# Two-layer graph network and mixture of experts: the router one tile slot earlier, two tiles picked at once and loaded three slots ahead, rows normalised in place, and another order of the lead groups

## The chip, the cores and the metric

One core of a Trainium2 chip. The metric is the device time of one launch in microseconds; the median of three runs stands for the kernel.

## The reference, cut to what matters

`x` has 10000 rows (nodes, later tokens) of 512 numbers. Two relational graph layers come first, then a mixture of experts on the normalised result.

```python
h   = relu(rgcn_gate_layer(layernorm(x), ...))        # x @ root + bias + sum over 5000 edges
x   = x + rgcn_gate_layer(h, ...)                      # second layer
t   = layernorm(x)
shared = sum over 2 experts of gelu(t @ sw1.T + sb1) @ sw2.T + sb2
probs  = softmax(t @ gate_w.T + gate_b)                # 8 routed experts
top_v, top_i = top_k(probs, 2)                         # the two best, with their shares
routed = sum over those two of top_v * (gelu(t @ rw1.T + rb1) @ rw2.T + rb2)
x   = x + shared + routed
```

## The kernel before, in words

**Stages.** The two graph layers take the first 931 us of the span: node tiles of 128 rows through `root`, 42 edge tiles through the relation weights, results added to `y1` and `z` in DRAM. The last 11 node tiles of layer 2 ("late2", loop over `late2_steps`) are multiplied after the edges. Then comes the mixture of experts, and that is where the change lies.

**Groups.** Tokens go through the router in 20 groups `q` of 512 (4 tiles of 128 rows in a partition). `load_group` (SP's queue) loads `x` into `zr`, `add_z` (POOL's queue, an accumulating DMA) adds `z`; `q_stats` (DVE) takes mean and variance; `group_rstd` (POOL) the factors; `q_norm` (ACT) writes the normalised rows to `stage`; `q_transpose` (PE) with `q_full` (ACT) turns them; `logits` and `logits_by_token` (PE), with `q_logits` (ACT) between them, give 8 logits for each token; `route_a`, an exponential in `q_exp` (ACT) and `route_b` (DVE) give the two best shares; `sort_kinds` (DVE) says which of 6 kinds (pairs of expert halves) a token is of; `count_ranks` (PE) counts ranks; `positions` (DVE) gives each token its row in the DRAM table `sorted_rows`, and `sort_rows` (POOL, 4 indirect DMAs) writes the rows there.

**Slots.** The experts work on 45 tiles of 256 sorted rows, one in each slot `i`. `pick_tile` (DVE) picks the kind with most rows; `load_tile` (SP) waits for the pick and for the sorting of all groups that it may read, and loads `xt[i % 4]`. A slot has `turn_tile` (transposes of the tile, PE; `f_hi`/`f_lo` split them on ACT and DVE), `up_routed` (26 matmuls), `up_shared` (12), the Gelu on ACT, `weigh` on DVE, `turn_hidden` (4 transposes), `down_first` (8), `down_routed` (12), `f_out` on DVE and `store_tile` (POOL, 2 indirect DMAs to `out`). PE's order in a slot is up_routed, up_shared, turn_tile of the next tile, [logits, counts, two q_transposes], turn_hidden, down_first, the third part of turn_tile, [two q_transposes, logits_by_token], down_routed.

**What sets the order.** Each engine runs its own list in program order; semaphores tie them. Groups 0 to 4 (lead groups) are routed before slot 0, partly between late2 steps. Groups 5 to 19 share the slots: every second slot turns, ranks and sorts one, so two slots and one group make a pair. `group_at(i, offset)` gives the group whose turn a step is in slot `i`; the last group is ranked in slot 31, and slots 32 to 44 have no group. The picks for slots `i + 2` and `i + 3` are made in the odd slot `i` that ranks a group, and `load_tile` is called two slots ahead:

```python
for i in range(NF):
    if exists(i + 2):
        load_tile(i + 2)
```

In the late2 steps DVE makes the router's small tables (`router_tiles`, which waits until the last edge rows are scattered) in step 2 and takes group statistics in steps 3, 5 and 8.

Of the kernel before, what the change touches and what calls it, by code (L numbers as in the profile page):

```python
# [63 lines left out]
def gnn_moe_kernel(nc, x, src, dst, etype, basis, att, gate_w, root, bias,  # L64
# [60 lines left out]
    with ctx:  # L125
# [63 lines left out]
        gbias = sb("gbias", [P, NE])  # L189
# [6 lines left out]
        kinds = sb("kinds", [P, 5, NKIND])  # L196
        rank_base = sb("rank_base", [P, QT, NKIND])
        lim_base = sb("lim_base", [P, NKIND])
        limt_base = sb("limt_base", [P, NKIND])
# [59 lines left out]
        zr, z1 = place("zr", [P, 2, QT, H], at=q1)  # L259
# [4 lines left out]
        seen = sb("seen", [P, 2, NKIND], BF16)  # L264
        is_kind = sb("is_kind", [P, 3 + QT, NKIND], BF16)
        pos = sb("pos", [P, 3, QT], I32)
        lim = sb("lim", [P, 2, NKIND])
        limt = sb("limt", [P, 2, NKIND])
        pick = sb("pick", [P, NF, 5])
# [3 lines left out]
        pick_one = sb("pick_one", [P, NKIND])  # L273
        pick_all = sb("pick_all", [P, 5, NKIND])
# [3 lines left out]
        stage, g1 = place("stage", [P, 3, QT, XW], at=xe_at)  # L278
# [19 lines left out]
        lgs = sb("lgs", [P, QT, NE])  # L298
# [4 lines left out]
        lg = sb("lg", [P, QT, NE])  # L303
        lg2 = sb("lg2", [P, QT, NE])
        mx = sb("mx", [P, QT])
        ex = sb("ex", [P, QT, NE])
        sm = sb("sm", [P, QT])
        rc = sb("rc", [P, QT])
        pr = sb("pr", [P, QT, NE])
        mx8 = sb("mx8", [P, QT, 8])  # L310
        topv = sb("topv", [P, QT, 8])
        rest = sb("rest", [P, QT, NE])
        cw = sb("cw", [P, QT, NE])
        cwh = sb("cwh", [P, QT, NE], F32R)
        qvar = sb("qvar", [P, 2, QT])
        held = sb("held", [P, QT, 4])
        has = sb("has", [P, QT, 4])
        half = sb("half", [P, QT, 2])
        newly = sb("newly", [P, NKIND])
# [83 lines left out]
        s_zin = [sem(f"x_loaded{i}") for i in range(2)]  # L403
        s_zadd = [sem(f"z_added{i}") for i in range(2)]
# [15 lines left out]
        s_sorted = [sem(f"rows_sorted{i}") for i in range(3)]  # L420
# [138 lines left out]

        LATE2_GROUP = NC * P // (QT * P)  # L560
# [26 lines left out]
        def turned_in_slot(i):  # L587
            return group_at(i, 9)

        def routed_in_slot(i):  # L590
            q = (i + 8) // 2
            return q if i % 2 == 0 and LEAD_GROUPS - 1 <= q < NQ else None

        def ranked_in_slot(i):
            q = (i + 7) // 2
            return q if i % 2 == 1 and LEAD_GROUPS - 1 <= q < NQ else None

        def picked_in_slot(i):

            q = ranked_in_slot(i)  # L600
            if q is not None:
                return [t for t in (i + 2, i + 3) if t < NF]
            return [i + 3] if i >= 2 * NQ - 8 and i + 3 < NF else []

        TURNS = [("a", 0), ("b", 0), ("x", 0)]
        for slot in range(NF):
            q = turned_in_slot(slot)
            TURNS += [("a", slot + 1), ("b", slot + 1)] if slot + 1 < NF else []
            TURNS += [(0, q), (1, q)] if q is not None else []
            TURNS += [("g", slot)]  # L610
            TURNS += [("x", slot + 1)] if slot + 1 < NF else []
            TURNS += [(2, q), (3, q)] if q is not None else []
# [8 lines left out]
        def wait_turn_bank(eng, part, n):  # L621
# [5 lines left out]
            if place_ < 3:  # L627
                eng.wait_ge(s_lo, 2 * (NT + ET))
                return
# [23 lines left out]
        def _(sp):  # L653
# [113 lines left out]
            def load_moe_small():  # L767
                sp.dma_start(gw[:], moe_gate_wT.rearrange("(k p) e -> p k e", p=P)).then_inc(s_sm2, 16)
                sp.dma_start(gbias[:], moe_gate_b.rearrange("(a e) -> a e", a=1).to_broadcast([P, NE])).then_inc(s_sm2, 16)
# [47 lines left out]
            def load_group(q):  # L817
                wait(sp, s_qn, QT * (q - 1))
                sp.dma_start(zr[:, q % 2, 0:tiles_of(q), :], q_rows(x, q)).then_inc(s_zin[q % 2], 16)

            def load_tile(i):
                q = group_of_pick(i)
                sp.wait_ge(s_pick, i + 1)
                for k in range(3):
                    wait(sp, s_sorted[k], 16 * sum(tiles_of(n) for n in range(k, q + 1, 3)))
# [9 lines left out]
            load_group(0)  # L835
            load_up_experts()
            load_group(1)
            for g in range(NG - 1, NG + 1):
                sp.wait_ge(s_tp, Step(SE, Pos(2 * (g - 4) + 1)).T.k + 1)
                load_pair(SE, Pos(g))  # L840
            for q in range(2, 6):
                load_group(q)
# [3 lines left out]
            load_tile(1)  # L846
            for i in range(NF):
                if exists(i + 2):
                    load_tile(i + 2)
                q = group_at(i, 14)  # L850
                if q is not None and q > 6:
                    load_group(q)
# [5 lines left out]
        def _(pool):  # L858
# [20 lines left out]
            pool.wait_ge(s_pool, 10)  # L879
# [13 lines left out]
            pool.wait_ge(s_pool, 15)  # L893
# [7 lines left out]
            pool.wait_ge(s_pool, 19)  # L901
            pool.sem_inc(s_const, 1)

            def kind_tables():
# [6 lines left out]
                iota(rank_base[:], [[0, QT], [KIND, NKIND]], HEAD + FW)  # L911
                iota(lim_base[:], [[KIND, NKIND]], HEAD)
                iota(limt_base[:], [[1, NKIND]], 0)
# [3 lines left out]
                iota(again_row[:], [[1, QLAST]], 0, QLAST)  # L917
                for k, (a, b, slot) in enumerate(KINDS):
                    for row, value in ((1, slot), (2, a + 1), (3, b + 1)):
                        pool.memset(kinds[:, row, k:k + 1], float(value)).then_inc(s_pool, 1)  # L920
                pool.wait_ge(s_pool, 19 + 26)
                pool.tensor_scalar(limt_base[:], limt_base[:], 0.125, None, ALU.mult).then_inc(s_pool, 1)
                same_rows = QT * P * (NQ - 1) - (N - QLAST * P)
                pool.tensor_scalar(valid[:], again_row[:], float(same_rows), None, ALU.is_ge).then_inc(s_pool, 1)
                pool.wait_ge(s_pool, 19 + 28)
                pool.tensor_tensor(limt_base[:], limt_base[:], lim_base[:], ALU.add).then_inc(s_pool, 1)
                pool.wait_ge(s_pool, 19 + 29)
# [141 lines left out]
            def group_extras(q):  # L1069
                s, n = q % 2, tiles_of(q)  # L1070
                high, low = (stage[:, q % 3, 0:n, SHARES + 3 * NR2 - 2 + k] for k in range(2))
                mean = qmv[:, s, 0:n, 0]
                if q < 3:
                    pool.wait_ge(s_qs, 1)
                else:
                    pool.wait_ge(s_sorted[q % 3], 16 * QT * (q // 3))
                pool.tensor_tensor(stage[:, q % 3, 0:n, STD], qvar[:, s, 0:n], qrstd[:, s, 0:n], ALU.mult).then_inc(s_qx, 1)
# [4 lines left out]
            def add_z(q):  # L1082
                if q == LATE2_GROUP:
                    late2_added(pool)
                pool.wait_ge(s_zin[q % 2], 16 * (q // 2 + 1))
                pool.dma_start(zr[:, q % 2, 0:tiles_of(q), :], q_rows(z, q),
                               accum_op=ALU.add).then_inc(s_zadd[q % 2], 16)

            def sort_rows(q):
                s, n = q % 2, tiles_of(q)  # L1090
                pool.wait_ge(s_qpos, q + 1)
                tokens = stage[:, q % 3, 0:n, TOKEN]
# [6 lines left out]
                for j in range(n):  # L1099
                    pool.indirect_dma_start(out=sorted_rows, in_=stage[:, q % 3, j, :], in_offset=None,  # L1100
                                            out_offset=bass.IndirectOffsetOnAxis(ap=pos[:, q % 3, j:j + 1], axis=0))\
                        .then_inc(s_sorted[q % 3], 16)
# [21 lines left out]
            add_z(0)  # L1124
            add_z(1)
            add_late2(LATE2_PAIRS[0])
            group_rstd(0)
            group_extras(0)
            add_late2(LATE2_PAIRS[1])
            group_rstd(1)  # L1130
            group_extras(1)
            add_z(2)
            add_late2(LATE2_PAIRS[2])
            add_late2(LATE2_PAIRS[3])
            add_z(3)
            group_rstd(2)
            add_late2(LATE2_PAIRS[4])
            sort_rows(0)
# [1132 lines left out]
```

## Time and profile before

| | us |
|---|---|
| median of 3 runs (lowest, highest) | 1766.83 (1765.28, 1771.9) |
| the profiled execution | 1758.73 |
| its span | 1757.0 |
| PE busy in the span | 1523.2 (87%) |
| DVE, ACT, POOL busy | 963.2, 711.8, 655.9 |

The profile is of one execution. The span runs from the first to the last instruction; 1.7 us of the execution lie around it. Slots are told apart by the Gelu of line 1355, one in each slot.

### The profile page before, as it was taken

The numbers are of one execution on the slowest core, as the hardware profiler recorded it, in microseconds if no ns is written. First come the engines' busy times: TensorE is split into PE (matmuls) and PEld (weight loads), VectorE is DVE, ScalarE is ACT, GpSimd is POOL, SyncE is SP. The second block draws the span as 40 slices with busy tenths as digits, with TensorE's granted clock in tenths as the row PEclk, the third lists the DMA queues.
The fourth block names the chain that finished last, engine by engine and source line by source line (L and its number), as shares of the span: only waits on it lengthen the run. The fifth ranks groups of instructions, "written<-read, shape, count | busy, mean of one in ns | idle before, by whom it ended". The sixth has DMA issues, their size and how long they took to land. (4 is left out here: it accounts for less than half of the span.)

```text
span 1757.0 us, 27836 instructions
## 1 busy us (share of the span) xinstructions
PE 1523.2 (87%) x8640; PEld 1216.1 (69%) x8640; DVE 963.2 (55%) x2837; ACT 711.8 (41%) x1232; POOL 655.9 (37%) x988
## 2 busy tenths in 40 slices
PE   7999999889979999999996736788788778878997
PEld 5777667777856777788875525676676667767886
DVE  5555777767523333466643565566465556645553
ACT  3334345556511112256652433454354345432331
POOL 3752142567530000026653344344334434432222
PEclk9999999999999999999998868999899999999999
DMA  9999997977689999967768855555545545432220
GB/s 245 272 282 306 281 308 231 292 133 121 95 200 288 280 278 278 300 187 124 136 105 185 204 162 163 162 159 155 181 132 173 175 148 156 132 103 98 100 75 17
DMA packets 115238, 325.96 MB, mean 186 GB/s; under 512 B 17244, under 2 KB 17770, under 8 KB 109859
## 3 DMA queue, kind: packets, MB, share of 16 engines
q1 hardware_dynamic: 77202, 211.19, 40.5%
q0 software_dynamic: 37904, 113.12, 28.0%
q8 instruction: 70, 1.15, 0.3%
q14 instruction: 62, 0.50, 0.1%
HBM read 205.63 MB, written 121.74 MB: 186 GB/s over the span
## 5 line engine op out<-in xcount | busy, mean ns | idle before, releaser
L1192 ACT ACTIVATE th<-bank 128x512 fp32r<-128x512 f32 x158 | 94.1, 596 | 284.8 <-PE bank L1467 284.6
L1120 POOL DMA_INDIRECT out<-xt,out_row x90 | 91.9, 1021 | 187.9 <-DVE xt L2169 169.6
L1812 DVE SCALAR_TENSOR_TENSOR tl<-bank,th 128x512 fp32r<-128x512 f32 x79 | 54.5, 690 | 190.9 <-ACT th L1192 190.8
L1447 PE MATMUL bank<-root2h,th 128*128 128x512 f32 x316 | 134.5, 425 | 18.3 <-DVE tl L1812 15.6
L984 POOL DMA_INDIRECT gx<-y,dst_slot x42 | 45.4, 1082 | 266.5 <-ACT xn_e L1212 242.6
L1447 PE MATMUL bank<-root1h,th 128*128 128x512 f32 x316 | 133.2, 422 | 7.2 <-DVE yout L1841 4.5
L1447 PE MATMUL bank<-root2l,th 128*128 128x512 f32 x316 | 127.2, 402 | 0.0
L1447 PE MATMUL bank<-root1l,th 128*128 128x512 f32 x316 | 126.5, 400 | 0.0
L1447 PE MATMUL bank<-root2h,tl 128*128 128x512 f32 x316 | 126.2, 400 | 0.0
L1447 PE MATMUL bank<-root1h,tl 128*128 128x512 f32 x316 | 125.6, 397 | 0.0
L1614 PE MATMUL bank<-ident,xt 128*128 128x128 f32 x360 | 57.7, 313 | 77.1 <-DMA xt<-sorted_rows 77.1
L1841 DVE TENSOR_TENSOR yout<-bank,bias_b 128x512 f32<-128x512 f32 x152 | 103.7, 682 | 26.2 <-DMA y<-yout 10.3
L1815 DVE TENSOR_TENSOR tl<-bank,th 128x512 fp32r<-128x512 f32 x79 | 54.4, 689 | 93.6 <-ACT th L1192 93.0
L1614 PEld LDWEIGHTS bank<-ident,xt 128*128 128x128 f32 x360 | 47.6, 161 | 80.6 <-DMA xt<-sorted_rows 80.6
L1447 PE MATMUL bank<-w1qh,tth 128*128 x360 | 101.6, 282 | 1.0 <-DVE ttl L2149 1.0
L1447 PE MATMUL bank<-w1ql,tth 128*128 x360 | 101.9, 283 | 0.0
L1447 PE MATMUL bank<-w1qh,ttl 128*128 x360 | 101.9, 283 | 0.0
L1480 PE MATMUL bank<-same,eh 128*128 128x256 f32 x336 | 84.3, 288 | 16.9 <-issue 9.2
L2149 DVE TENSOR_TENSOR ttl<-bank,tth 128x512 fp32r<-128x512 f32 x90 | 59.1, 685 | 72.3 <-ACT tth L1344 71.5
L999 POOL DMA_INDIRECT z<-msg,scat_slot x42 | 70.5, 1678 | 64.1 <-issue 64.1
L1100 POOL DMA_INDIRECT sorted_rows<-stage,pos x79 | 81.0, 1025 | 27.4 <-issue 14.2
L1355 ACT ACTIVATE gelr<-bank 128x512 f32<-128x512 f32 x45 | 26.9, 598 | 157.3 <-PE bank L1633 157.2
(292 smaller groups left out, 4490.3 us busy)
## 6 DMA issues: line engine op xcount, KB each, us to landing
basis_t<-in_gnn_basis SPq DMA_DIRECT2D x64, 896.0 KB
xt<-sorted_rows SPq DMA_DIRECT2D x45, 560.0 KB, 4.0
xin<-in_x SPq DMA_DIRECT2D x39, 512.0 KB, 8.7
xin<-y SPq DMA_DIRECT2D x39, 512.0 KB, 8.1
zr<-in_x SPq DMA_DIRECT2D x19, 1024.0 KB, 5.2
zr<-z POOLq DMA_DIRECT2D x19, 1024.0 KB, 8.1
y<-yout SPq DMA_DIRECT2D x37, 512.0 KB, 8.9
z<-yout SPq DMA_DIRECT2D x34, 512.0 KB, 7.7
```

What stands on the lines that cost most here:

```text
L984: pool.indirect_dma_start(out=gx[:, e % 6, :], out_offset=None, in_=x if pr.phase == SB else y1, in_offset=bass.IndirectOffsetOnAxis(ap=ds ...
L999: pool.indirect_dma_start(out=y1 if pr.phase == SB else z, out_offset=bass.IndirectOffsetOnAxis(ap=scat_slot[:, t:t + 1], axis=0), in_=msg ...
L1100: pool.indirect_dma_start(out=sorted_rows, in_=stage[:, q % 3, j, :], in_offset=None, out_offset=bass.IndirectOffsetOnAxis(ap=pos[:, q % 3 ...
L1120: pool.indirect_dma_start(out=out, in_=xt[i % 4][:, j, 0:H], in_offset=None, out_offset=bass.IndirectOffsetOnAxis(ap=out_row[:, i % 4, j:j ...
L1192: act.activation(th_a[:, s, :], tpb[s][:], f).then_inc(s_hi, 1)
L1447: ins = pe.matmul(out_ap, a(k), b(k), start=first, stop=last)
L1480: pe.matmul(o, eh[:, j, k * P:(k + 1) * P], m, start=j == 0, stop=False)
L1614: ins = pe.transpose(b[:, k * FW + j * P:k * FW + (j + 1) * P], t[:, j, (first + k) * P:(first + k + 1) * P], ident[:])
L1812: ins = dve.scalar_tensor_tensor(out=tl_a[:, s, :], in0=tpb[s][:], scalar=0.0, in1=th_a[:, s, :].bitcast(F32), op0=ALU.max, op1=ALU.subtract)
L1815: ins = dve.tensor_tensor(tl_a[:, s, :], tpb[s][:], th_a[:, s, :].bitcast(F32), ALU.subtract)
L1841: dve.tensor_tensor(target, out_bank(st)[:], bias_b[st.layer][:], ALU.add).then_inc(s_y, 1)
L2149: dve.tensor_tensor(to[0], turn_bank(part, i)[:], to[1].bitcast(F32), ALU.subtract).then_inc(s_flo, 1)
```

## The change: what it does

- `ranked_in_slot` gives a group to the even slot `(i + 8) // 2` instead of the following odd one; `routed_in_slot` moves to the odd slot before it, `turned_in_slot`, statistics, loads and adds move one slot earlier relative to the group. The two picks of a group are for slots `i + 3` and `i + 4`, and `load_tile` is called three slots ahead.
- `zr` goes. `x` and `z` are loaded and added straight into four `stage` buffers of 560 numbers a row, the statistics are taken there, and `q_norm` works in place. `load_group` waits for the sorting of the group four before.
- The router bias is added in `q_logits`; the top two are taken from the logits and the exponential is taken of both the logits and the logits without the top two; the tensor `seen` of counts goes, running limits are kept in `lim` by DVE. `route_a` has one more step (max and match), `route_b` and `sort_kinds` have fewer.
- PE's order in a slot becomes up_routed, count_ranks, two q_transposes, logits, up_shared, turn_hidden, turn_tile of the next tile, logits_by_token, down_first, two q_transposes, down_routed 0, third part of turn_tile, the register loads of the next pick, down_routed 1. In ACT's list `q_full` 0 and 1 and `q_logits` stand behind the first Gelu, `routed_hi` ahead of `f_hi`. In DVE's `positions` stands behind `weigh`, `routed_lo` ahead of `f_lo`, `route_a`, picks, `route_b` and `sort_kinds` at the end.
- Lead groups: all four loads and adds go ahead of late2's adds; `router_tiles` is in late2 step 5, statistics in steps 6 and 8 (and the others behind the last), group 0 is turned ahead of step 9; groups 1 to 3 follow step 10, with `positions(q - 1)` behind `route_a(q)`; group 4 is turned and routed ahead of slot 0 and ranked in it.

```diff
         def turned_in_slot(i):
-            return group_at(i, 9)
+            return group_at(i, 10)
 
         def routed_in_slot(i):
-            q = (i + 8) // 2
-            return q if i % 2 == 0 and LEAD_GROUPS - 1 <= q < NQ else None
+            return group_at(i, 9)
 
         def ranked_in_slot(i):
-            q = (i + 7) // 2
-            return q if i % 2 == 1 and LEAD_GROUPS - 1 <= q < NQ else None
+            q = (i + 8) // 2
+            return q if i % 2 == 0 and q < NQ else None
...
-                return [t for t in (i + 2, i + 3) if t < NF]
-            return [i + 3] if i >= 2 * NQ - 8 and i + 3 < NF else []
+                return [t for t in (i + 3, i + 4) if t < NF]
+            return [i + 4] if i > 2 * NQ - 10 and i + 4 < NF else []
...
             def load_group(q):
-                wait(sp, s_qn, QT * (q - 1))
-                sp.dma_start(zr[:, q % 2, 0:tiles_of(q), :], q_rows(x, q)).then_inc(s_zin[q % 2], 16)
+                wait(sp, s_sorted[q % 4], 16 * QT * (q // 4))
+                sp.dma_start(stage[q % 4][:, 0:tiles_of(q), 0:H], q_rows(x, q)).then_inc(s_zin[q % 4], 16)
...
-                if exists(i + 2):
-                    load_tile(i + 2)
+                if exists(i + 3):
+                    load_tile(i + 3)
...
             def q_norm(q):
                 s = q % 2
                 act.wait_ge(s_qst, q + 1)
-                wait(act, s_sorted[q % 3], 16 * QT * (q // 3))
-                wait(act, s_qtp, KC * (q - 1))
...
-                    act.activation(stage[:, q % 3, j, 0:H], zr[:, q % 2, j, :], ACT.Identity, bias=qnmr[:, s, j:j + 1],
+                    act.activation(rows, rows, ACT.Identity, bias=qnmr[:, s, j:j + 1],
...
                 ins.then_inc(s_upr, 1)
-                up_shared(i)
-                if exists(i + 1):
-                    turn_tile(i + 1, "a")
-                    turn_tile(i + 1, "b")
-                if q_route is not None:
-                    logits(q_route)
                 if q_rank is not None:
                     count_ranks(q_rank)
                 if q_turn is not None:
                     q_transpose(q_turn, 0)
                     q_transpose(q_turn, 1)
+                if q_route is not None:
+                    logits(q_route)
+                up_shared(i)
                 turn_hidden(i)
-                chunks = [pe.value_load(pick_int[0:1, i, c:c + 1], min_val=1, max_val=FC - 1) for c in (2, 3)]
+                if exists(i + 1):
+                    turn_tile(i + 1, "a")
+                    turn_tile(i + 1, "b")
+                if q_route is not None:
+                    logits_by_token(q_route)
                 for j in range(2):
                     down_first(i, j)
-                if exists(i + 1):
-                    turn_tile(i + 1, "x")
                 if q_turn is not None:
                     q_transpose(q_turn, 2)
                     q_transpose(q_turn, 3)
-                if q_route is not None:
-                    logits_by_token(q_route)
-                for j in range(2):
-                    down_routed(i, j, chunks)
+                down_routed(i, 0, chunks)
+                if exists(i + 1):
+                    turn_tile(i + 1, "x")
+                    chosen = picked(i + 1)
+                down_routed(i, 1, chunks)
...
-                if e == 2:
+                if e == 5:
                     router_tiles()
-                if e in (3, 5, 8):
-                    q_stats({3: 0, 5: 1, 8: 2}[e], range(QT))
...
+                if e == 6:
+                    q_stats(0, range(QT))
+                if e == 8:
+                    q_stats(1, range(QT))
...
                 for t in picked_in_slot(i):
                     pick_tile(t)
...
                 if q_route is not None:
-                    route_a(q_route)
                     route_b(q_route)
+                    sort_kinds(q_route)
```

## Rows read from the trace of the kernel before

**Rows 1.** The page: span, and PE's busy tenths in 40 slices of 43.9 us.

```profile
span 1757.0 us, 27836 instructions
...
PE   7999999889979999999996736788788778878997
```

**Rows 2.** Busy time of each engine by stretch, granted clock, DMA share, GB/s.

```profile
955.00:1010.00 55.00, 37.76 (x173) 27.97 (x173) 28.46 (x87) 21.15 (x35) 18.25 (x31) 0.79 0.87 202
1010.00:1053.00 43.00, 15.73 (x96) 10.13 (x94) 28.58 (x145) 15.23 (x28) 18.18 (x30) 0.64 0.61 166
...
1105.00:1605.00 500.00, 407.96 (x2643) 341.14 (x2641) 288.60 (x1158) 223.39 (x381) 200.66 (x363) 0.94 0.49 149
1300.30:1333.60 33.30, 27.30 (x178) 22.70 (x178) 19.48 (x79) 15.36 (x26) 14.01 (x25) 0.95 0.54 165
...
1650.00:1694.50 44.50, 43.84 (x291) 39.39 (x291) 22.82 (x64) 13.33 (x28) 11.90 (x25) 1.00 0.26 86
```

**Rows 3.** The Gelu of line 1355, slots 0 to 10 and 32 to 44.

```profile
L1355 ACT ACTIVATE gelr<-bank x11: 597/598/598, 1068.5 to 1230.8; 128x512 f32<-128x512 f32 x11
...
L1355 ACT ACTIVATE gelr<-bank x13: 598/598/598, 1601.2 to 1739.0; 128x512 f32<-128x512 f32 x13
```

**Rows 4.** Waits from 1105 to 1605 us: total, times, longest.

```profile
PEld bank L1614 <- DMA xt<-sorted_rows: 61.6, 14, 5.6
```

**Rows 5.** DMA issues of the same stretch: count, KB, median us to landing.

```profile
xt<-sorted_rows SPq DMA_DIRECT2D x28, 560.0 KB, 4.4
...
zr<-z POOLq DMA_DIRECT2D x11, 1024.0 KB, 8.1
...
sorted_rows<-stage,pos POOLq DMA_INDIRECT x59, 4.2
```

**Rows 6.** PE in one pair of slots: start, us, what, idle before.

```profile
1304.43 1.22 PE L1614 MATMUL bank<-ident,xt 128*128 128x128 f32 x8 [4.13 <-DMA xt<-sorted_rows]
1305.58 1.93 PE L1581 MATMUL bank<-tfull,gwp 128*32 128x512 f32 x8
```

**Rows 7.** ACT in the same pair.

```profile
1311.16 1.28 ACT L1338 ACT_TABLE_LOAD   x1
...
1313.03 2.94 ACT L1319 ACTIVATE stage<-zr,qnmr,qrstd 128x512 f32<-128x512 f32 x4 [0.34 <-POOL qnmr L1067]
```

**Rows 8.** DVE in the same pair.

```profile
1311.20 0.29 DVE L2056 TENSOR_REDUCE lgs<-bank 128x32 f32<-128x128 f32 x1 [0.27 <-PE bank L1588]
...
1317.97 0.17 DVE L2109 TENSOR_TENSOR seen<-seen,newly 128x6 bf16<-128x6 bf16 x1
1319.36 0.76 DVE L2155 TENSOR_TENSOR gelr<-gelr,xt 128x256 f32<-128x256 f32 x2 [1.22 <-issue]
```

**Rows 9.** PE in a slot without a group.

```profile
1657.95 0.28 PE L1447 MATMUL bank<-w1qh,tth 128*128 x1
...
1661.06 0.28 PE L1447 MATMUL bank<-tth,w1sh 128*128 128x256 f32 x1
...
1662.51 1.03 PE L1614 MATMUL bank<-ident,xt 128*128 128x128 f32 x8
1663.38 0.60 PE L1646 MATMUL bank<-ident,gelr 128*128 128x128 f32 x4
1664.12 0.50 PE L1655 MATMUL bank<-b2r,cwt 128*128 128x512 f32 x1
...
1666.22 0.48 PE L1447 MATMUL bank<-w2h,grh 128*128 x1
```

**Rows 10.** DVE in such a slot: its first operation.

```profile
1662.02 0.76 DVE L2155 TENSOR_TENSOR gelr<-gelr,xt 128x256 f32<-128x256 f32 x2 [3.12 <-ACT gelr L1355]
```

**Rows 11.** PE from late2 to slot 0: first instruction after three long idle times.

```profile
955.51 0.80 PE L1447 MATMUL bank<-root2h,th 128*128 128x512 f32 x1 [10.54 <-DVE tl L1812]
...
1045.59 1.12 PE L1588 MATMUL bank<-ident,lgt 128*128 128x128 f32 x4 [10.91 <-ACT lgt L1333]
...
1069.90 1.97 PE L1614 MATMUL bank<-ident,xt 128*128 128x128 f32 x8 [11.56 <-DMA xt<-sorted_rows]
```

More of the change, by code:

```diff
@@ L823, in load_tile @@
                 sp.wait_ge(s_pick, i + 1)
-                for k in range(3):
-                    wait(sp, s_sorted[k], 16 * sum(tiles_of(n) for n in range(k, q + 1, 3)))
+                for k in range(4):
+                    wait(sp, s_sorted[k], 16 * sum(tiles_of(n) for n in range(k, q + 1, 4)))
                 if i < 4:
@@ L1332, in q_logits @@
                 wait(act, s_lgx, q)
[L1333 removed]
+                act.activation(lgt[:, 0:n], bank[7][:, 0:n], ACT.Identity, bias=gbias[:, 0:1]).then_inc(s_lgt, 1)
             def q_exp(q):
@@ L1409, in _ @@
             f_shares(0)
+            for k in range(KC):
+                q_full(4, k)
+            q_logits(4)
+            q_exp(4)
             q_norm(5)
@@ L2101, in sort_kinds @@
[L2101 to L2104 removed]
+                left = held[:, 0:n, 0:2].rearrange("p j (a b) -> p j a b", b=1).to_broadcast([P, n, 2, 2])
@@ L2180, in _ @@
                     expert_lo(FC + e - 2)
-                if e == 2:
+                if e == 5:
                     router_tiles()
-                if e in (3, 5, 8):
-                    q_stats({3: 0, 5: 1, 8: 2}[e], range(QT))
-                if e == 7:
-                    route_a(0)
-                    route_b(0)
-                    sort_kinds(0)
-                if e == 9:
-                    positions(0)
-            for q in range(1, 4):
-                route_a(q)
-                if q < 3:
-                    q_stats(q + 2, range(QT))
-                route_b(q)
-                sort_kinds(q)
-                if q < 3:
-                    positions(q)
-                if q == 2:
-                    pick_tile(0)
-                    bias_rows()
-            for part in ("a", "b"):
-                f_lo(0, part)
+                if e == 6:
+                    q_stats(0, range(QT))
+                if e == 8:
+                    q_stats(1, range(QT))
+            q_stats(2, range(QT))
+            route_a(0)
+            route_b(0)
+            sort_kinds(0)
+            q_stats(3, range(QT))
+            route_a(1)
+            positions(0)
+            route_b(1)
+            sort_kinds(1)
+            route_a(2)
+            positions(1)
+            route_b(2)
+            sort_kinds(2)
+            route_a(3)
+            positions(2)
+            pick_tile(0)
+            route_b(3)
+            sort_kinds(3)
+            bias_rows()
             positions(3)
@@ L2206, in _ @@
             pick_tile(2)
+            q_stats(4, range(QT))
+            for part in ("a", "b"):
+                f_lo(0, part)
+            route_a(4)
             q_stats(5, range(QT))
+            route_b(4)
+            sort_kinds(4)
             for i in range(NF):
-                q_route, q_rank, q_first, q_more = routed_in_slot(i), ranked_in_slot(i), group_at(i, 11), group_at(i, 10)
+                q_route, q_rank, q_first, q_more = routed_in_slot(i), ranked_in_slot(i), group_at(i, 12), group_at(i, 11)
                 if i:
@@ L2212, in _ @@
                         f_out(i - 1, j)
-                if q_rank is not None and q_rank > 3:
-                    sort_kinds(q_rank)
                 if q_more is not None and q_more > 5:
-                    q_stats(q_more, range(1, 3))
+                    q_stats(q_more, range(2, QT))
                 chunks = [dve.value_load(pick_int[0:1, i, c:c + 1], min_val=1, max_val=FC - 1) for c in (2, 3)]
@@ L2219, in _ @@
                     weigh(i, c, chunks[c])
+                if q_rank is not None:
+                    positions(q_rank)
                 shared_lo(i)
+                routed_lo(i)
                 if exists(i + 1):
@@ L2223, in _ @@
                     f_lo(i + 1, "b")
-                routed_lo(i)
-                if q_rank is not None:
-                    positions(q_rank)
+                if q_route is not None:
+                    route_a(q_route)
                 for t in picked_in_slot(i):
```

402 lines of the change are left out of this document (187 added, 215 removed).

## The prediction

> **What bounds the kernel now.** I read the page first: PE is busy 87% of the span, but its row of tenths is at 9 in most slices of the graph layers, falls to 6, 7, 3 in the three slices from about 922 us and stays at 7 or 8 for the next thirteen, then 9 again [rows 1]. So two stretches have slack, and the change touches only these. The table by stretch gives their size: from 1105 to 1605 us PE is busy 408.0 of 500 us at a granted clock of 0.94, DVE 58%, ACT 45%, POOL 40%; from 1650 us, in slots without a group, PE is busy 43.84 of 44.5 us at clock 1.00 [rows 2]. Nothing is saturated in the first and PE is in the second: the first is a latency loop. The Gelu of line 1355 marks the slots: slot 0 at 1068.5, slot 32 at 1601.2, slot 44 at 1739.0 us [rows 3]. So 32 slots took 532.7 us, 33.3 a pair of slots with a group; the last 12 took 137.8.
>
> Which wait ends last? PE's weight loads waited 61.6 us for `xt<-sorted_rows` in 14 pairs, up to 5.6 us each [rows 4]; in the pair I follow the wait was 4.13 us, and the transposes and logits behind it ran slow (8 transposes 1.22, logits 1.93 us; 8 transposes at full clock take 1.03) [rows 6, 9]. The tile is late for a reason seen in the code: `positions` of the odd slot, 4 sort DMAs of about 1.3 us issue each, 4.2 us until the last lands, then 4.4 us for the tile [rows 5], and PE wants the tile in the next slot.
>
> **The pair after the change.** PE's own work first. In a slot without a group [rows 9]: up_routed 1657.95 to 1661.06, 3.11; up_shared 1.45; 8 transposes and turn_hidden 1.61; down_first with the third part 2.10, so about 0.235 a matmul and 2.82 for the 12 of down_routed; sum 11.1 us. A group adds 16 transposes (8 in 0.87), 1.75; logits, half of the slow 1.93, 0.97; 4 transposes 0.44; counts about 0.15 by my estimate (bounds 0 and 0.5): 3.3. Pair: 2 x 11.1 + 3.3 = 25.5 us. Cross-check: the pair before was 27.30 busy [rows 2], and the two slow pieces above hold 1.3 of it, so 26.0. I take 25.5.
>
> Does the tile come in time? From the start `U` of the work behind up_routed in the even slot: `positions` ends near U + 4.5; POOL first stores the tile before (2.6), computes rows (1.2) and issues an add (1.0), then sorts (tokens 0.7, 4 x 1.3), last issue near U + 10.5, landed U + 14.7; SP's registers 1.0; tile landed near U + 20. PE turns tile `i + 3` in slot `i + 2`, near U + 29.5. Nine us to spare, so the 61.6 us go, and with them the slow pieces. The ring through the group's own loads is as safe: `load_group` now waits for the sorting of the group four before, then load (about 5), add 8.1 [rows 5], statistics and turn, some 25 us of DMA and queue for a distance of eight slots, 105 us. Writing rows of 2048 bytes at a pitch of 2240 in place of 8192 bytes in a run costs the loads something that no row shows; bounds 0 and 4 us each (double the 4.4 us of a tile, which is in runs of 4480), hidden by the same 7 to 9 us.
>
> What is late next? The exponential. In the odd slot PE turns the tile's third part only behind half of down_routed. From there to the next turn_hidden ACT has: share copy 0.4, table load 1.28, exp 0.23, q_norm 2.94, table load 1.28, Gelu 0.60 [rows 3, 7], then DVE's weigh 0.76 [rows 8], with 0.3 of handovers 7.8 us. PE has down_routed 1 1.41, up_routed 3.11, counts 0.15, two q_transposes 0.87, up_shared 1.45 = 7.0. Stall 0.8 us. DVE's way round is near the same: from route_a to the end of the kinds 1311.20 to 1318.14 = 6.9 us, less f_out's 1.4 and a wait of 0.5, 5.0 of work [rows 8]; about 2.1 of it (route_b, sort_kinds) follows the exp, then f_out 1.4, register loads 1.22, weigh 0.76, with copy, load, exp and handover 2.0 ahead: 7.4. The kinds are ready 4.2 us after the third part, PE asks for them 4.5 after it: they are just in time. In the even slot two picks (1.45 each before, one operation of 0.25 less now), statistics and f_out end about when the next Gelu does: no stall. Pair 25.5 + 0.8 = 26.3; ends 25.5 (chains hidden) and 29.5 (both chains 1.6 us longer and a stall in the even slot too). I take 26.3, because each piece is from a row.
>
> [...] Rows 7 show 1.28 us, and the exponential behind it begins at once. [...]
>
> **Slots without a group.** turn_hidden now follows up_shared at once. The first DVE operation of such a slot starts at 1662.02 and the weighing ends at 1662.78 [rows 10], up_shared ends at 1662.51 [rows 9]: 0.3 us of stall and a handover, less a register load that moves; 11.45 a slot. The transposes of the next tile no longer cover it. That is +0.35 x 13 = 4.5 us, with bounds 0 and 8.
>
> **The lead.** PE idled 10.54 us at step 4 (behind the router's tables, which waited for the last edge scatter), 10.91 and 11.56 us later [rows 11]; from 955 to 1053 it was busy 53.5 of 98 us, at clock 0.79 and 0.64 [rows 2]. With the tables in step 5, steps 4 to 8 (3.2 us each, a little slower at low clock) run from about 950 to 969; the weights' load sits behind one more megabyte, so not earlier. Group 0's statistics wait for its add (issued 953.8, 8.1 us), q_norm 0 ends near 970, its turn 974, step 9, logits, step 10: late2 ends near 982, not 1009. Then three groups at about 10 us each, one after another: q_norm 2.94, turn 4, logits 1.9, copy 0.6, turn back 0.6: 1012. Behind them: pick 0, bias rows 6, positions 3 near 1026, sort and land 9.5, while group 4 has load, add (8.1), statistics, q_norm, turn, logits until 1046. First up_routed near 1046 instead of 1053.5. Slot 0's Gelu then waits for route_a 4, statistics 5 (2.5) and q_norm 5: about 1057 instead of 1068.5. The four adds at once, with two of late2 behind them, are the weak point: bounds 1045 and 1075.
>
> **Sum.** Slot 0 at 1057; 31 slots to slot 31, the last beside a group's ranks, 15.5 x 26.3 = 407.7, 1464.7; 13 slots of 11.45, 148.9, 1613.6 for slot 44 (before 1739.0); the tail of 18.0 stays: span 1631.6, execution 1633.3 with the 1.7 around it. The profiled execution, 1758.73, stands 8.1 below the median 1766.83, so I add that: 1641.4.
>
> **Rivals.**
> - *The in-order chain of ACT and DVE bounds the pair at about 29.5 us.* For: the two chains are already 0.4 to 0.8 over PE's and meet in one place. Against: the waits before showed them hidden. 15.5 x 3.2 = 50: 1691. Chance 0.17. [...]
> - *The lead groups don't gain,* because the adds queue up and q_norm 0 and late2's buffers wait for them: slot 0 near 1071, pair 26.3. 1655. Chance 0.17.
> - *The tile is still late* (it doesn't do what it says): sort and load would need 9 us more. DMA busy share was 0.49 and would be about 0.62. Pair 32: 1730. Chance 0.04.
> - *Slower than before.* `count_ranks` now stands first behind up_routed and waits for `sort_kinds`, behind the exp, behind the third part. If the kinds come 9 us late in each pair, the pair is 35.3, 15.5 x 9.0 = 140 more: 1781. It decides from (1767 - 1641) / 15.5 = 8.1 us of lateness on; by my sum the kinds are 0.3 early. Chance 0.02, with another 0.01 for a lead that blocks outright.
> - *Better:* chains hidden, lead 8 us earlier: 1641 - 12 - 8 = 1621. Chance 0.12.
>
> **How the numbers follow.** The forecast, 1641, has the rest, 0.47. Range 1615 to 1700: it holds the better case, the first two rivals and the bounds, and leaves out the last ones and the tails. Faster by over 0.5% (about what a measurement of this kernel tells from no change, 8.8 us): 0.95; within: 0.02; slower: 0.03.
>
> **What would show it.** Right: hardly a wait of PE for `xt<-sorted_rows`; a Gelu pitch of 26 to 27 us a pair, the even slot longer; PE 96% busy there at clock near 1.0; turn_hidden waiting 0.5 to 1 us for `weigh` in even slots and 0.3 in the last 13, which then take 11.4 to 11.5; the last late2 step near 982; slot 0's Gelu near 1057. Wrong: PE waiting at L1594 for the kinds or at the group's transposes for q_norm, DVE's weigh waiting on register loads, the granted clock still near 0.94 in the pairs, or q_stats 0 waiting far past 965 for its add.

## The result, and the profile after

The changed kernel takes 1664.08 us (median of 4 runs, 1654.27 to 1665.64) beside 1767.23 us for the kernel before on the same chip: ratio 0.940, 95% interval 0.936 to 0.944. Measured once more on another chip it took 1652.53 us beside 1760.45: ratio 0.938, 0.936 to 0.941. The forecast was 1641 us, its range 1615 to 1700.

The profiled execution took 1665.64 us, its span 1663.9. Here are the page's busy times, and the rows of tenths for PE and its clock:

```profile
span 1663.9 us, 27765 instructions
...
PE 1506.3 (91%) x8680; PEld 1211.2 (73%) x8680; DVE 928.8 (56%) x2663; ACT 704.9 (42%) x1230; POOL 661.5 (40%) x989
...
PE   6999998989998999999999774399999999999997
...
PEclk9999999989999999999999985599999999999999
```

The thirteen slices of 6 to 8 in [rows 1] (the first of them is a 6, which the prediction reads as 7 or 8) are now 9. The hole ahead of them is still there, with two slices of the clock at half speed. The table by stretch, columns as in [rows 2]:

```profile
955.00:1010.00 55.00, 35.88 (x158) 26.07 (x159) 31.43 (x105) 20.29 (x34) 17.79 (x32) 0.78 0.77 145
1010.00:1053.00 43.00, 15.45 (x93) 9.91 (x92) 25.07 (x137) 12.10 (x21) 21.78 (x28) 0.50 0.72 209
...
1105.00:1495.00 390.00, 368.93 (x2586) 318.83 (x2585) 253.17 (x981) 213.08 (x372) 198.63 (x351) 1.00 0.61 184
1550.00:1594.50 44.50, 43.76 (x292) 39.38 (x290) 22.43 (x61) 13.73 (x29) 11.78 (x24) 1.00 0.27 90
```

In the slots with groups PE goes from 82% busy at clock 0.94 to 95% busy at 1.00. From 955 to 1053 us it was busy 53.5 us before and is busy 51.3 now: nothing was gained there. The Gelus that mark slots 0, 16, 17, 18, 31, 32 and 44, in the order of [rows 3]:

```profile
1083.37 0.60 ACT L1348 ACTIVATE gelr<-bank 128x512 f32<-128x512 f32 x1
...
1303.06 0.60 ACT L1348 ACTIVATE gelr<-bank 128x512 f32<-128x512 f32 x1
...
1317.37 0.60 ACT L1348 ACTIVATE gelr<-bank 128x512 f32<-128x512 f32 x1 [6.45 <-PE bank L1619]
...
1330.45 0.60 ACT L1348 ACTIVATE gelr<-bank 128x512 f32<-128x512 f32 x1
...
1502.87 0.60 ACT L1348 ACTIVATE gelr<-bank 128x512 f32<-128x512 f32 x1 [5.55 <-PE bank L1619]
1513.93 0.60 ACT L1348 ACTIVATE gelr<-bank 128x512 f32<-128x512 f32 x1 [4.10 <-PE bank L1619]
...
1646.68 0.60 ACT L1348 ACTIVATE gelr<-bank 128x512 f32<-128x512 f32 x1 [4.10 <-PE bank L1619]
```

Slot 0 is 14.8 us later than before; this pair takes 27.4 us (1303.06 to 1330.45), the mean of the 14 pairs from slot 2 to 30 is 27.1, beside 33.6 before by the same mean; slot 44 is 92.3 us earlier, nearly all of what the span lost (93.1).

**What is left in a pair.** PE's waits in the even slot 16, each row with the idle time before it, and PE's waits summed from 1105 to 1480 us (total, times, longest):

```profile
1301.81 1.09 PE L1556 MATMUL bank<-ident,stage1q 128*128 128x128 f32 x8 [0.19 <-ACT stage1q L1312]
1304.64 0.66 PE L1632 MATMUL bank<-ident,gelr 128*128 128x128 f32 x4 [0.32 <-DVE gelr L2135]
...
1311.63 0.49 PE L1430 MATMUL bank<-w2h,grh 128*128 x1 [1.13 <-issue]
```

```profile
PE bank L1430 <- issue: 11.3, 11, 1.2
PE bank L1632 <- DVE gelr L2135: 7.0, 20, 1.4
PE bank L1556 <- ACT stage2q L1312: 0.7, 4, 0.2
```

The wait for the tile [rows 4] doesn't appear any more. In its place stands a hole of 1.13 us behind the register loads for the next tile, once a pair, in the even slot. ("issue" means that the profile shows nothing that PE waited for.)

**What happened in the lead.** PE's first instruction after each long idle time, as [rows 11]:

```profile
992.13 0.80 PE L1430 MATMUL bank<-root2h,th 128*128 128x512 f32 x1 [7.04 <-DVE tl L1796]
1004.21 1.97 PE L1556 MATMUL bank<-ident,stage1q 128*128 128x128 f32 x8 [5.80 <-ACT tfull L1320]
...
1052.87 1.97 PE L1600 MATMUL bank<-ident,xt 128*128 128x128 f32 x8 [15.58 <-DMA xt<-sorted_rows]
1064.07 3.77 PE L1556 MATMUL bank<-ident,stage0q 128*128 128x128 f32 x16 [8.81 <-ACT stage0q L1312]
```

Two of these lead to the order of POOL's queue. The first begins with DVE, which couldn't write late2's next piece because its buffer wasn't free; POOL had issued four adds of 1 MB ahead of the one of 512 KB that frees it. The fourth begins with group 4's rstd, behind an add that waited for its x:

```profile
987.42 0.69 DVE L1825 TENSOR_TENSOR yout<-bank,bias_b 128x512 f32<-128x512 f32 x1 [13.33 <-DMA z<-yout]
```

```profile
960.33 1.29 POOL L1085 DMA_DIRECT2D stage0q<-z  x1 [6.68 <-issue]
...
962.69 2.64 POOL L1085 DMA_DIRECT2D stage3q<-z  x1
963.44 3.69 POOL L1055 DMA_DIRECT2D z<-yout  x2
...
1057.70 1.32 POOL L1085 DMA_DIRECT2D stage2q<-z  x1 [8.54 <-DMA stage2q<-in_x]
1059.09 0.22 POOL L1062 TENSOR_SCALAR qvar<-qmv 128x4 f32<-128x4 f32 x1
```

### The profile page after: what moved, and what is told of

It is laid out like the page before. It is cut to its first block and busy times, and to the rows that moved or that the text cites. A ratio compares the mean times of both kernels' runs of the same rounds, so it can differ in the third digit from the quotient of the medians.

```text
span 1663.9 us, 27765 instructions
## 1 busy us (share of the span) xinstructions
PE 1506.3 (91%) x8680; PEld 1211.2 (73%) x8680; DVE 928.8 (56%) x2663; ACT 704.9 (42%) x1230; POOL 661.5 (40%) x989
## 5 line engine op out<-in xcount | busy, mean ns | idle before, releaser
L2135 DVE TENSOR_TENSOR gelr<-gelr,xt 128x256 f32<-128x256 f32 x90 | 34.3, 423 | 107.7 <-ACT gelr L1348 106.6
L1000 POOL DMA_INDIRECT y<-msg,scat_slot x42 | 70.1, 1668 | 55.6 <-issue 53.4
L1430 PEld LDWEIGHTS bank<-root2h,th 128*128 128x128 f32 x316 | 61.6, 195 | 33.6 <-DVE tl L1796 16.6
L1430 PE MATMUL bank<-w2h,grh 128*128 x180 | 75.6, 420 | 11.3 <-issue 11.3
```

The source lines that it names most:

```text
L1000: pool.indirect_dma_start(out=y1 if pr.phase == SB else z, out_offset=bass.IndirectOffsetOnAxis(ap=scat_slot[:, t:t + 1], axis=0), in_=msg ...
L1430: ins = pe.matmul(out_ap, a(k), b(k), start=first, stop=last)
L2135: dve.tensor_tensor(part, part, share.to_broadcast([P, 2, 2, P // 2]), ALU.mult).then_inc(s_gs, 1)
```

## The experiments

Each is timed beside the kernel before; the ratio is to that.

**1. Does the wait from sorting to tile load bound the pair?** The kernel before, one line changed:

```
-            return min(NQ - 1, (i + 5) // 2)
+            return min(NQ - 1, (i + 5) // 2 - (4 <= i < 33))
```

> The kernel before, with the tiles of slots 4 to 32 picked by the counts of one group earlier, so that their loads wait only for rows that were sorted two slots before (which rows the tiles hold differs from the reference; the work is the same). Theory (sorting to tile load bounds the pair): PE's 61.6 us of waits for the tile go with nothing else changed, the pair falls from 33.3 to between 27 and 29 us, 15 pairs, so 60 to 90 us faster, time 1680 to 1705. Rival (order of the work on PE, ACT and DVE is what counts): the tile is only what came last; the pair stays over 31 us and less than 30 us is gained.

1688.93 us, ratio 0.960 (0.955 to 0.966): 72.6 us faster. The pair falls to 28.7 us (mean of 14, from the Gelus), and from 1105 to 1480 us PE waits for the tile 11.8 us, where the kernel before has 50.0 in the same stretch:

```profile
PE bank L1573 <- DVE ttl L2149: 15.8, 13, 1.6
PE bank L1614 <- DMA xt<-sorted_rows: 11.8, 11, 1.9
```

Distance alone, with the old order of every engine, gives over two thirds of the gain: slots 0 to 31 take 447.9 us, beside 518.1 before and 412.5 to 419.5 in the changed kernel. The wait of 15.8 us for `ttl` (the turn buffer, not yet free) is one piece of what remains of the old order; the changed one hasn't got it. The prediction's first step stands.

**2. The four adds ahead of late2's.** The changed kernel with

```
+            add_z(0)
+            add_z(1)
             add_late2(LATE2_PAIRS[0])
             add_late2(LATE2_PAIRS[1])
+            add_z(2)
+            add_z(3)
```

in place of the four `add_z` first.

> The changed kernel with the first two additions of late2's pieces issued ahead of the third and fourth group's x + z, instead of behind them. Theory (queued adds): in the changed kernel the first y_out piece (512 KB) landed 23.9 us after its issue because four adds of 1 MB stood in the queue; with two of them ahead it lands near 975 instead of 987, PE's wait of 7 us for its low half goes, late2's last step ends 8 to 11 us earlier (near 988) and slot 0's Gelu comes 8 to 10 us before 1083.4; time 1654 to 1656. Rival (latency further on): group 2's and 3's rows come later, or the loads of tile 0 and group 4 bind, and slot 0's Gelu moves by less than 2 us; time within 2 us of the changed kernel's. The slots' pitch is the same in both.

1646.99 us, ratio 0.936 (0.931 to 0.942). DVE's wait for the piece, then PE:

```profile
974.25 0.69 DVE L1827 TENSOR_TENSOR yout<-bank,bias_b 128x512 f32<-128x512 f32 x1 [2.56 <-DMA z<-yout]
```

```profile
982.05 0.66 PE L1575 MATMUL bank<-ident,lgt 128*128 128x128 f32 x4 [0.81 <-ACT lgt L1328]
...
992.15 1.97 PE L1558 MATMUL bank<-ident,stage1q 128*128 128x128 f32 x8 [5.80 <-ACT tfull L1322]
```

The 13.33 us became 2.56 and the 7.04 are gone; late2's last step ends at 985.3, not 997.4, and slot 0's Gelu comes at 1071.7, 11.7 us earlier. Late2 began 0.9 us earlier in this execution (935.7 for 936.6), so some 11 us are the move's; experiment 9 shows how far such a difference scatters. Its last step also ran at 0.23 us a matmul, not 0.43: behind the idle time the granted clock was 0.51 (from 992.1 to 997.4 us), here it was 1.00 (from 982.4 to 985.3), which is 12 x 0.2 = 2.4 us of the gain. The rival (later links bind) fell. Late2's adds of `yout` (count, KB, median landing), in the changed kernel and then here:

```profile
z<-yout POOLq DMA_DIRECT2D x3, 512.0 KB, 23.9
```

```profile
z<-yout POOLq DMA_DIRECT2D x3, 512.0 KB, 15.2
```

Here the adds landed in the order of their issue: 8.6, 13.4, 16.1 (the two of late2), 21.6 and 26.0 us after it. With four adds of 1 MB issued ahead of them late2's first took 23.9 us to landing, with two 15.2, and DVE's wait for it fell from 13.33 to 2.56 us.

**3. Group 4's rstd behind the add of group 6.** The changed kernel with

```
             for q in range(4):
                 sort_rows(q)
-                if q:
+                if q in (1, 2):
                     add_z(q + 3)
             group_rstd(4)
             group_extras(4)
+            add_z(6)
```

> The changed kernel with group 4's rstd and extras ahead of the x + z add of group 6 on POOL's queue. Theory (in-order queue): in the changed kernel group 4's variance was ready near 1049, but POOL stood for 8.5 us at the add of group 6, whose x landed at 1057.7, and rstd came behind it; moved ahead, q_norm 4 starts near 1053, group 4's transposes 8 us earlier, slot 0's Gelu 5 to 8 us before 1083.4, time 1657 to 1660. Rival (the next link takes over): slot 0's Gelu waits for route_a 4, stats 5 and q_norm 5, and these for the add of group 5 or for DMA; Gelu 0 moves by less than 2 us and the time stays.

1647.10 us, ratio 0.935 (0.930 to 0.940). POOL's rows here:

```profile
1048.13 0.22 POOL L1062 TENSOR_SCALAR qvar<-qmv 128x4 f32<-128x4 f32 x1
...
1056.73 1.35 POOL L1085 DMA_DIRECT2D stage2q<-z  x1 [6.07 <-DMA stage2q<-in_x]
```

rstd 4 comes 11 us earlier, PE's wait of 8.81 us for group 4's rows is gone, slot 0's Gelu is at 1071.3, 12.1 earlier. Not all of that is the move's: PE turned tile 0, whose rows are sorted ahead of the place that was changed, at 1051.53 in this execution and at 1052.87 in the other. From there to slot 0's Gelu it took 30.5 us and takes 19.8, so the move is worth 10.7 us, more than the 5 to 8 expected: the in-order tail of ACT, `q_norm 4`, exp 4 and `q_norm 5`, moves with it. The rival fell. Both moves belong to one mistake: what an issuing engine holds up behind a DMA that isn't urgent.

**4. The hole behind the register loads.** The changed kernel with `chosen = picked(i + 1)` moved from behind the third part of the tile to right behind `down_first`.

> The changed kernel with PE's three register loads for the next tile issued right behind down_first, ahead of the group's last eight transposes, instead of between the third part's transposes and the second half of down_routed. Theory (register latency): the hole of 1.13 us ahead of down_routed 1 in even slots is the time the loads take with one short set of transposes queued ahead; placed earlier it goes in even slots, the pair is 26.3 instead of 27.4 us and the time falls by 12 to 17 us. Rival (sequencer bound): PE's own issue is the limit behind the loads wherever they stand, so the hole only moves to the place behind down_first; pair 27.4, time within 3 us. A third way: the odd slot has fewer transposes between and gets a hole it had not, pair unchanged.

1654.43 us, ratio 0.940 (0.935 to 0.944): no gain that can be told. The trace says why. The hole of each pair is gone (PE's waits for "issue" 11.3 us to 0.3), the mean pair from slot 2 to 30 is 26.2 us, beside 27.1 and 26.7. But in slots without a group no transposes follow the loads, `down_routed` comes at once, and such a slot takes 11.31 us where it took 11.06: 3 us given back. Slots 0 to 31 took 406.1 us, beside 419.5 and 412.5 in the two profiled executions of the changed kernel (experiment 5). So the theory was right on the hole and too high on its worth: 6 to 13 us in the pairs, 3 lost behind them. The third way is seen in the slots without a group. Why the loads cost anything in the even slot isn't shown: in the changed kernel's odd slots and slots without a group they stand behind the same two transposes and six matmuls and leave no hole. What the even slot has besides is eight of the group's transposes ahead of `down_routed`.

**5. The changed kernel once more.**

> The changed kernel itself, beside the others of this call. Expected: slot 0's Gelu within 3 us of 1083.4, the pitch of a pair 27.0 to 27.5 us and the same hole behind the register loads, once a pair. If it is the edge stage that makes slot 0 move between executions, the late2 steps move with it; a rival is that the slots' pitch moves from one execution to the next, and then the 1.1 us over the forecast is not a fixed cost.

1652.53 us, ratio 0.938. Slot 0's Gelu is at 1084.2, the mean pair from slot 2 to 30 is 26.7 us, where the first execution has 27.1; the hole behind the register loads is the same (11.3 us in all). The second part of the expectation failed: the pitch isn't the same in two executions. First the odd slot 15 in the first execution, its last up-projection on PE, and then ACT's Gelu; below, the same in this one:

```profile
1288.52 0.28 PE L1619 MATMUL bank<-b1r,cwt 128*128 x1
...
1289.98 0.60 ACT L1348 ACTIVATE gelr<-bank 128x512 f32<-128x512 f32 x1 [6.67 <-PE bank L1619]
```

```profile
1287.65 0.28 PE L1619 MATMUL bank<-b1r,cwt 128*128 x1
...
1287.97 0.60 ACT L1348 ACTIVATE gelr<-bank 128x512 f32<-128x512 f32 x1 [5.64 <-PE bank L1619]
```

ACT starts 1.18 us after the matmul's end in one, 0.04 in the other, in odd slots only, and in the first PE's wait for `gelr` is 7.0 us in all against 4.2. What holds ACT is not in the trace; it stays open. Slots 0 to 31 took 7.0 us more in the execution that has it (419.5 for 412.5), of which PE's wait for `gelr` accounts for 2.8. Of the nine profiled executions of the changed kernel and its variants three have it: this first one and those of experiments 8 and 10.

**6. How much slack has ACT's chain?** The changed kernel with two one-column activations (result unused) behind the exponential of a group:

```
                     q_exp(q_route)
+                    act.activation(unused[:, 0:1], minus_half[:, 0:1], ACT.Gelu)
+                    act.activation(unused[:, 1:2], minus_half[:, 0:1], ACT.Exp)
```

> The changed kernel with two one-column activations (a Gelu, an Exp; their result isn't used) behind each group's exponential in the slots' loop: two more table loads of 1.28 us and about 0.2 us each for the activations, some 3 us more on ACT once a pair. [...] Rival (ACT has slack): PE's wait grows by less than 1 us a pair, the time by less than 15 us.

1713.18 us, ratio 0.975 (0.970 to 0.980): 60.7 us slower than the changed kernel beside it. ACT and PE in one pair:

```profile
1314.46 1.28 ACT L1332 ACT_TABLE_LOAD   x1
1315.76 0.26 ACT L1332 ACTIVATE ex<-lg 128x64 f32<-128x64 f32 x1
1316.03 1.28 ACT L1417 ACT_TABLE_LOAD   x1
1317.33 0.20 ACT L1417 ACTIVATE unused<-minus_half 128x1 f32<-128x1 f32 x1
1317.53 1.28 ACT L1418 ACT_TABLE_LOAD   x1
1318.83 0.20 ACT L1418 ACTIVATE unused<-minus_half 128x1 f32<-128x1 f32 x1
1318.94 2.91 ACT L1313 ACTIVATE stage1q<-stage1q,qnmr,qrstd 128x512 f32<-128x512 f32 x4
```

```profile
1321.90 1.09 PE L1559 MATMUL bank<-ident,stage1q 128*128 128x128 f32 x8 [3.19 <-ACT stage1q L1313]
```

2.91 us were put in, and PE's wait for the group's rows went from 0.19 to 3.19: no slack at all, as I had expected (a pair 2.5 to 3 us longer, 35 to 45 us in all), but the place is the group's transposes, and I had named `turn_hidden`, which waits for `gelr` behind them. The pair grew by 3.7 us (slots 0 to 31: 470.1 beside 412.5, over 15.5 pairs), so 0.7 more than the wait; that rest, and the 12 us between 49.1 (the spans) and 60.7 (the medians), I can't place. Four times in a row a table load takes 1.28 us and the activation follows 0.02 us or less behind it.

**7. Run length of the loads.** The kernel before, with `(q j p) d -> q p j d` for `(q p j) d -> q p j d`.

> The kernel before, with the four rows of a partition taken 128 rows apart instead of side by side, so that the x and z loads of a group move in runs of 2 KB instead of 8 KB (token numbers in the output then belong to other rows; work and sizes are the same). Theory (run length): the x load's landing goes from about 5.1 us to the 7.5 to 8 us that the changed kernel shows, and as it is hidden the time stays within 5 us. Rival (crowding): the landing stays near 5 us, and what made it longer in the changed kernel is that the queues hold more at that moment. The add of z, written through the software queue, should stay near 8 us if its price is set by the accumulation.

1776.57 us, ratio 1.009 (1.006 to 1.012): 16.1 us slower, where at most 5 were expected. From 1105 to 1480 us (count, KB, median landing):

```profile
zr<-in_x SPq DMA_DIRECT2D x10, 1024.0 KB, 5.5
zr<-z POOLq DMA_DIRECT2D x10, 1024.0 KB, 9.4
sorted_rows<-stage,pos POOLq DMA_INDIRECT x42, 5.2
```

The load goes from 5.1 to only 5.5 us, so 2 KB runs at the source don't explain the 7.5 to 8.1 of the changed kernel, where the destination too is in 2 KB pieces and more is in flight; which of these two it is wasn't separated. The theory fell. The add grew by 1.3 us and the sort by 0.8 (from 4.4 in the same stretch), and the pair by 1.4. That fits a loop in which every part of a microsecond between add and tile reaches PE, but which of the two growths reached it wasn't tested.

**8. The cover that the slots without a group lost.** The changed kernel, with the next tile's eight transposes ahead of `turn_hidden` in slots 33 to 44, as before, and ACT's and DVE's operations in the same order.

> The changed kernel with the order of the kernel before in the slots without a group (33 to 44): the next tile's first eight transposes ahead of turn_hidden, and the operations of ACT and DVE behind them in the same order. Theory (cover): turn_hidden waits 0.19 us in each of these slots in the changed kernel; with 0.87 us of transposes ahead of it this wait goes, a slot takes 10.9 instead of 11.07 us and the time falls by about 2 us. Rival (the cover is paid for elsewhere): the low half of the hidden rows comes later, down_routed waits, the slot takes 11.1 us or more and the time doesn't fall.

1669.57 us, ratio 0.948 (0.943 to 0.952). A slot takes 12.04 us, not 11.06, and the last 13 together 154.5, not 143.8. PE's waits in one:

```profile
1590.67 0.49 PE L1433 MATMUL bank<-w2h,grh 128*128 x1 [0.16 <-DVE grl L2150]
1592.99 0.49 PE L1433 MATMUL bank<-w2h,grh 128*128 x1 [0.45 <-issue]
```

The 0.19 us for `gelr` went; a wait for `grl` came, and behind it the register loads show. The rival held: in the changed kernel this order costs 10.7 us. It doesn't follow that the cover was a loss before. There such a slot took 11.10 us with it, PE didn't wait for `grl`, and the register loads stood elsewhere; so the loss belongs to the cover together with the changed kernel's other order, and which part of that makes it wasn't separated.

**9. The three repairs together:** experiments 2 and 3, and the loads early only in slots with a group's transposes.

```
                 if q_turn is not None:
+                    following = picked(i + 1)
                     q_transpose(q_turn, 2)
...
-                    chosen = picked(i + 1)
+                    chosen = picked(i + 1) if q_turn is None else following
```

> The changed kernel with both moves in the lead (two additions of late2 ahead of the adds of groups 2 and 3; group 4's rstd ahead of the add of group 6) and with the register loads ahead of the group's last eight transposes, but only in slots that have them; in the slots without a group they stay where they were. Theory (three separate costs): the lead gains 12 us by the first and up to 8 more by the second, so slot 0's Gelu at 1062 to 1066; the pair 26.2 to 26.4 us; slots without a group 11.08; time 19 to 31 us under the changed kernel's, 1630 to 1642. Rival (one common limit in the lead): the two moves there give 12 us together, slot 0 near 1071, because each shows by itself the same limit, DMA or the wait for tile 0; time 1643 to 1648.

1625.11 us (1621.69 to 1628.81), ratio 0.923 (0.920 to 0.926), beside 1652.53 of the changed kernel on the same chip: 27.4 us faster than it and 135.3 faster than the kernel before. Slot 0's Gelu is at 1059.9, the mean pair 26.04 us, slots without a group 11.06:

```profile
1105.00:1460.00 355.00, 347.88 (x2436) 300.63 (x2435) 239.05 (x942) 200.29 (x349) 189.88 (x329) 1.00 0.63 193
```

PE is busy 98% of it. Late2 began at 931.4 in this execution. Counted from there, slot 0's Gelu takes 128.5 us, beside 146.8 and 146.6 in the changed kernel's two, 136.0 in experiment 2 and 133.1 in experiment 3: the two moves give 18.3 us together where they seem to give 10.8 and 13.6 alone, and the rest of the 24.3 us is the earlier start. The missing 6 us don't show an overlap of the two costs; they are within the scatter, as two stretches show. From PE's turn of tile 0 to slot 0's Gelu, where only the second move acts, the kernels without it take 29.5 to 33.9 us (six executions), those with it 19.8, 20.1 and 20.1 (experiments 3, 9 and 10). From late2's start to the turn of tile 0, where only the first acts, those without it take 113.0 to 116.4 us (six executions), those with it 105.0, 108.4 and 107.8 (experiments 2, 9 and 10). So the second move is worth some 10 us or more, the first 5 to 11, and so few executions can't say it closer.

**10. With the order of experiment 8 as well.**

> The version with the two moves in the lead and the earlier register loads, and with the order of e_turn in the slots without a group as well. Expected: slot 0's Gelu at 1058 to 1062, the pair 26.0 to 26.2 us, and a time 0 to 3 us under that version's 1625, so 1622 to 1626; if the rival of the last run holds, 1625 to 1629.

1650.98 us (1645.0 to 1660.06), 26 more than the version without it, far off both ends. The profiled executions differ by 28.2 us at slot 44's Gelu. 10.8 are the slots without a group (12.05 us each), 2.4 the lead. Slots 0 to 31 took 418.8 us against 403.9, though nothing in them was changed: here the late odd Gelu of experiment 5 is in nearly every pair, by 1.8 to 2.4 us. ACT's Gelu in one, and PE's wait for it:

```profile
1295.87 0.60 ACT L1351 ACTIVATE gelr<-bank 128x512 f32<-128x512 f32 x1 [5.99 <-remote]
```

```profile
1297.44 0.66 PE L1638 MATMUL bank<-ident,gelr 128*128 128x128 f32 x4 [0.89 <-DVE gelr L2145]
```

PE's waits for `gelr` come to 16.4 us in all (from 1090 to 1460 us), against 4.5 in experiment 9, so some 12 of these 14.9 us are the late Gelu's. The profile puts twelve of the late Gelus down to "remote", a releaser that it can't name; on-time ones it puts down to PE. Why this kernel shows it throughout is open.

## Why the prediction was right, and where it was wrong

The measured time lies inside the range, and the mechanism in the slots was right; the forecast of 1641 itself was 22.7 us too low. The forecast for slot 44's Gelu was 1613.6, it came at 1646.7: 33.1 us late. By the prediction's own terms: slot 0, 26.4 late (1083.4 for 1057); slots 0 to 31, 11.8 (419.5 for 407.7); the last 13, 5.1 early (143.8 for 148.9). The 8.1 us were added because the profiled execution before lay that far below its median; this one lay 1.6 above. That hid 9.7 us of the miss, and it was luck.

- **The tile in time: right.** No wait for it is left, and experiment 1 gets most of the gain from the distance alone.
- **The pair, 26.3: a term was missing.** Measured 27.1 and 26.7 (means; 27.4 for the pair shown), and 26.2 and 26.0 once the register loads stand earlier (experiments 4 and 9). The sum of the pair has no term for PE's register loads; they cost about 1.1 us in each even slot. The move is named only for the slots without a group, as a gain ("less a register load that moves").
- **ACT's chain at its edge: right in time, wrong in place.** [rows 7] priced it well: 0.2 us of wait for the group's rows and 0.3 for `gelr`, where 0.8 was forecast. Experiment 6 shows no slack. With 2.91 us more of chain the mean pair is 30.6, past the first rival's 29.5.
- **The table load: right.** It was taken as 1.28 us with the exponential at once behind it. After the change it is 1.28 us and the exponential begins 0.01 behind it (1324.76, 1326.05).
- **The lead: wrong, this is the step that failed.** "Late2 ends near 982" and "slot 0 about 1057" came out as 997.4 and 1083.4. The adds at once were named as the weak point and their price, "slot 0 near 1071", was given to the second rival; that was the truer one in mechanism, and still 12 us short (1083.4 lies outside the prediction's own bounds of 1045 and 1075), since a second block in the same queue (rstd 4 behind the add of group 6) wasn't seen at all. Counted from late2's start, both moves together return 18.3 us; the forecast needed 21.7 (125.1 for 146.8). The groups' own 10 us each were right (1012.4 to 1022.4). Late2 also began at 936.6 in place of 931.9; over the executions of all kernels here that start lies between 931.4 and 938.6, so whether the change has a part in it is open.
- **Slots without a group, 11.45: too dear.** 11.06 measured, 11.10 before. The loss of the cover, priced at +0.35 a slot, shows as 0.19 us of wait, and the hole of 0.17 us that the register loads left in their old place (behind `turn_hidden`) is gone.
- **x and z loads, 0 to 4 us more and hidden: right** in size (5.1 to about 7.8) and in the pairs; in the lead, where 10.8 to 12.8 us were seen, it wasn't hidden: the 8.54 us for which POOL's queue stood still (experiment 3) were a wait for one of them. The lead also had x loads of 6.4 us before (median of eight), so how much of this is the new layout isn't separated.

## What to carry to other kernels

When a change gathers DMA issues of one engine, list for each the first one that somebody waits for, and put it ahead of the large ones nobody waits for (here 13.33 us of wait became 2.56); the same goes for an operation that stands behind an issue which itself waits (8.54 us here). Register loads on PE's queue left a hole of 0.8 to 1.3 us in one slot and none in the next: look for the hole behind them in each kind of slot, and place them by what the trace shows. And in this latency loop across several engines distance alone gave over two thirds of the gain (experiment 1): widen first, then order what each engine does.

## What the runs showed of the hardware that was not expected

- A 512 KB add issued behind four of 1 MB landed after 23.9 us (the changed kernel), and after 15.2 us with two of 1 MB ahead of it (experiment 2); DVE's wait for it was 2.56 us in place of 13.33.
- Three register loads on PE left a hole of 0.8 to 1.3 us in the even slots with a group in the changed kernel and none in the others, behind the same two transposes and six matmuls; placed ahead of eight transposes they left 0.3 us in all. In experiment 8, where PE waits for `grl` ahead of them, they left 0.43 to 0.59 in slots without a group.
- Behind 7.04 us of idle time on PE the granted clock was 0.51 and the next twelve matmuls took 0.43 us each; in experiment 2, without that idle time, it was 1.00 and they took 0.23.
- The same program started its odd slots' Gelus some 1.2 us late in one execution and at once in another; a variant had them 1.8 to 2.4 us late.
